# A small product behind every TensorE step of the last two pairs

## The chip, the cores and the metric

The kernel runs on one NeuronCore of a Trainium2 chip. Its metric is the time of one execution on the device in microseconds, as the median of several runs. Five engines work side by side, each in its own program order: PE (matrix products into PSUM), DVE (vector work; it and ACT read PSUM), ACT (tanh and exp), POOL (masks and elementwise products in SBUF) and SP, which issues the transfers. They are tied together by semaphores: an instruction raises one when it is done, another engine waits until it has reached a number.

## What is computed

The input is x of 16 batches, 512 rows and 128 columns, all in fp32. A first layer is attention with 16 heads of 8 columns, causal, with normalized q and k and a soft cap of the scores; its output is added to x and normalized over the row. A second layer selects 63 of the 512 rows of each batch by a learned weight, runs attention and a feed-forward layer on those rows alone, scales them by their weight, and puts them back; the result is added and normalized once more. Cut to what matters:

```python
scores = jnp.tanh(scores / SOFTCAP) * SOFTCAP          # first layer
probs  = softmax(where(causal, scores, -inf))
x      = _layernorm(x + probs_times_v @ w_o.T)
weights = (x @ router_w)[..., 0] + router_b[0]         # second layer
sel_idx = sort(top_k(weights, 64)[1][:, :63])
x1   = x_sel + attention(rmsnorm(x_sel, ln1)) @ wo
x2   = x1 + gelu(rmsnorm(x1, ln2) @ w1) @ w2
out  = zeros.at[sel_idx].set(x2 * w_sel) + x * (1 - sel_mask)
x    = _layernorm(x + out)
```

## The kernel before

The 16 batches go in 8 pairs. The body runs for p from -1 to 10; each body has 16 steps of two half-steps, and at each half-step every engine does what a table written by hand lists for it (PE_ORDER, VE_ORDER, POOL_ORDER, ACT_ORDER). An entry such as `"late.sc0@-2"` names a function and the pair, relative to p, that it works on. `run_side` (L466) goes through the entries of one half-step and leaves out those whose pair does not exist. Between them stand the scores of the first layer: `scores` (L1142) writes them into the five banks of ps_s, ACT takes them from there with tanh (L684), then exp (L696), POOL masks them (L591), and PE multiplies with v (L1165).

The last scores are made in body 7. Bodies 8, 9 and 10 hold only what is left of the pairs 6 and 7, the stages of the second layer above all. Of these the prediction uses, in their order for one pair:

- `sel_gather` (L1233): picks the selected rows by products with a one-hot matrix E, two halves of 64 rows (k), each with 4 products of 129 columns (L1240) and 4 of 16 (L1242); its result goes through DVE to hn.
- `sel_hnT` (L1264), `sel_qkv` (L1269; rows L1272 and L1275), `sel_R` (L1250, row L1255), the mask product, and `sel_qkT` (L1289, row L1293).
- `att_scores` (L1296, row L1301), `att_P` (P0T and P1T, transposes through the helper `four`, L1172), `att_PV` (PV, L1315), `att_oT` (L1322), `att_wo` (L1327), `att_h2T` (L1332), `att_w1` (w1, L1338).
- `late_w2` (w2, L1345), and `late_sc` (L1349, row L1354), the scatter of the rows back to their places: late.sc0 for the first batch, from rows 0 to 63 of ET and proc into bank ps_a, late.sc1 for the second, from rows 64 to 127 into bank ps_m.

DVE follows nearly every one of them with a copy or a scaling, and PE's next step waits for that. PSUM has eight banks: five are ps_s, one is ps_y, and ps_a and ps_m serve all other stages in turn.

A product in fp32 shows as two records in the trace, a transpose as one.

Of the kernel before, what the change touches and what calls it, by code (L numbers as in the profile page):

```python
# [15 lines left out]
B, S, D = 16, 512, 128  # L16
# [6 lines left out]
PAIRS = B // 2  # L23
# [25 lines left out]
def moments_of(tiles, tag=""):  # L49
# [45 lines left out]
PE_ORDER = (  # L95
    ["att.S1@-2"], ["prep.qk0/1@0"],
    ["prep.qk1/1@0"], ["pv.3/1@-1", "prep.v/1@0"],
    ["fin.y1T/1@-1"], ["route.wrow/0@-1"],
    [], ["att.P0@-2", "pv.0/0@0", "att.P1@-2"],
    ["att.PV@-2"], ["fin.yT/1@-1", "att.oT@-2"],  # L100
    ["att.wo@-2", "fin.wo/1@-1"], [],
    ["prep.xT/0@1", "pv.1/0@0", "att.h2T@-2"], ["att.w1@-2", "prep.qk0/0@1"],
    ["route.wrow/1@-1"], ["prep.qk1/0@1"],
# [198 lines left out]
def build(nc, x, w_q, w_k, w_v, w_o, amask, pos, router_w, router_b, wq, wk, wv, wo, w1, w2, ln1, ln2, out):  # L302
    ctx = ExitStack()
    with ctx:
        def sb(name, shape, dt=F32):
            return ctx.enter_context(nc.sbuf_tensor(name, shape, dt))

        def sem(name):
            return ctx.enter_context(nc.semaphore(name))

        ident = sb("ident", [P, P])
# [16 lines left out]
        w1_sb = sb("w1_sb", [P, F])  # L329
# [89 lines left out]
        ps_s = ctx.enter_context(nc.psum_tensor("ps_s", [P, GROUP], F32))  # L419
# [17 lines left out]
        tanh_done = sem("tanh_done")  # L437
# [19 lines left out]
        def live(n, top):  # L457
            n = n.no if isinstance(n, Batch) else n
            return not isinstance(n, int) or 0 <= n < top

        def iterations(body):

            for p in range(-1, PAIRS + 3):
                body(p)

        def run_side(order, table, p, s, half):  # L466

            for entry in order[2 * s + half]:
                name, shift = entry.split("@")
                name, _, k = name.partition("/")  # L470
                unit = Batch(p + int(shift), int(k)) if k else p + int(shift)
                if live(unit, B if k else PAIRS):
                    table[name](unit, unit.k if isinstance(unit, Batch) else None)

        def group(p, s, lag=0):

            s -= lag
            b = Batch(p, s // 8)
            return (b, b.k, s % 8) if live(b, B) else None
# [72 lines left out]
        def _(pool):  # L552
# [60 lines left out]
            def sel_zb(q, _):  # L613

                ve["late"].wait(pool, q - 1, "z1")
                for k in range(2):
                    ve["route"].wait(pool, Batch(q, k), "coef")
                    pl["sel"].done(mul(z_base[:, k], x1[:, k, :, 0:D], coef[:, k, :, None].to_broadcast([P, NT, D])),
                                   f"zb{k}", q)

            def att_kw(q, _):
                ve["sel"].wait(pool, q, "qkT")
                pe["att"].wait(pool, q - 1, "PV")
                for k in range(2):
                    pl["att"].done(mul(
                        k_wide[:, k], qkT[:, 1, None, SLOTS * k:SLOTS * k + SLOTS].to_broadcast([P, H, SLOTS]),
                        head_of[:, :, None].to_broadcast([P, H, SLOTS])), f"kw{k}", q)
# [14 lines left out]
            def body(p):  # L642
                for s in range(16):
                    g = group(p, s, 1)
                    if g:
                        b, _, gi = g
                        pool.wait_ge(exp_done, b.no * 8 + (gi + 1))

                        nc.gpsimd.tensor_tensor(pool_mark[:, gi:gi + 1], head_of[:, 0:1], head_of[:, 0:1], ALU.mult)  # L649
                        causal(gi, 0, 1, 0, P)  # L650
                        causal(gi, 0, 2, 384, P)
                        causal(gi, 0, 3, 1024, 256)
                        causal(gi, 0, 2, 1920, P).then_inc(masked, 1)
                    for half in range(2):
                        run_side(POOL_ORDER, table, p, s, half)
# [4 lines left out]
        def _(act):  # L660
# [14 lines left out]
            def body(p):  # L675
                for s in range(16):
                    g = group(p, s)
                    if g:
                        b, _, gi = g
                        for u, (c0, c1) in enumerate(UNIT):  # L680
                            act.wait_ge(scores_ready, b.no * 16 + (2 * gi + u + 1))
                            if gi >= 2 or b.at_least(1):
                                act.wait_ge(exp_done, b.no * 8 + (gi - 1))
                            nc.scalar.activation(th[:, gi % 2, c0:c1], ps_s[:, c0:c1], ACT.Tanh,  # L684
                                                 scale=1.0 / (QK_SCALE ** 2 * DH ** 0.5 * SOFTCAP))\
                                .then_inc(tanh_done, 1)
                    for half in range(2):
                        run_side(ACT_ORDER, table, p, s, half)
                    g = group(p, s, 1)
                    if g:  # L690
                        b, _, gi = g
                        act.wait_ge(tanh_done, b.no * 16 + (2 * gi + 2))

                        if gi >= 4 or b.at_least(1):
                            act.wait_ge(pv_done, b.no * 4 + (gi // 2 - 1))
                        nc.scalar.activation(pr[:, gi % 4, :], th[:, gi % 2, :], ACT.Exp, scale=SOFTCAP)\  # L696
                            .then_inc(exp_done, 1)
# [4 lines left out]
        def _(v):  # L702
# [411 lines left out]
            def body(p):  # L1114
                for s in range(16):
                    for half in range(2):
                        run_side(VE_ORDER, table, p, s, half)
# [4 lines left out]
        def _(t_):  # L1122
            mm = nc.tensor.matmul
# [18 lines left out]
            def scores(b, k, gi, u):  # L1142

                if gi > 0 or b.at_least(1):
                    t_.wait_ge(tanh_done, b.no * 16 + (2 * gi + u - 1))
                for hb_, kb in UNIT_BLOCKS[u]:
                    g, j = 2 * (gi // 4) + hb_, gi % 4
                    c = COL[(hb_, kb)]
                    last = mm(ps_s[:, c:c + S - P * kb], k_st[32 * j:32 * j + 32, k, kb, g, :],  # L1149
                              q_st[32 * j:32 * j + 32, k, kb:NT, g, :], start=True, stop=True)  # L1150
                last.then_inc(scores_ready, 1)
# [197 lines left out]
            def late_sc(q, k):  # L1349
                ve["late"].wait(t_, q, "proc")  # L1350
                bank_free(f"late.sc{k}", q)
                rows = slice(SLOTS * k, SLOTS * k + SLOTS)
                for c in range(NT):
                    last = mm(at(f"late.sc{k}")[:, P * c:P * c + P], ET[rows, P * c:P * c + P], proc[rows, :], start=True, stop=True)  # L1354
                pe["late"].done(last, f"sc{k}", q)
# [10 lines left out]
                     "att.h2T": att_h2T, "att.w1": att_w1, "late.w2": late_w2,  # L1366
                     "late.sc0": lambda q, _: late_sc(q, 0), "late.sc1": lambda q, _: late_sc(q, 1)}

            def body(p):
                for s in range(16):  # L1370
                    for half in range(2):
                        g = group(p, s, -1)
                        if g and g[2] == 0 and half == 0:
                            t_.wait_ge(turned[g[1]], g[0].pair * 32 + 32)
                        if g:
                            scores(g[0], g[1], g[2], half)
                        run_side(PE_ORDER, table, p, s, half)
            iterations(body)

# [26 lines left out]
```

## Time and profile before

| | us |
|---|---|
| median of 3 runs (lowest, highest) | 842.22 (840.51, 843.31) |
| the profiled execution | 842.46 |
| its span on the core | 840.7 |
| PE busy, share of the span | 695.8, 83% |
| DVE busy | 615.0, 73% |
| ACT busy | 609.1, 72% |
| POOL busy | 420.1, 50% |

### The profile page before, as it was taken

What the parts mean: (1) busy time and instruction counts of PE and PEld (TensorE: products, weight loads), DVE (VectorE), ACT (ScalarE), POOL (GpSimd) and SP (SyncE); (2) the same over time, 40 slices, a digit from 0 to 9 for tenths busy, and PEclk for the clock granted to TensorE, in tenths of its full rate; (3) what the DMA queues carried; (4) which work ended last, traced back from release to release, by engine and by line L of the source; (5) the groups of instructions that cost most, each with busy time, mean ns of one, the idle gap of its engine ahead of it and who ended that gap; (6) DMA issues with size and microseconds to landing.
All of it is one profiled execution on the core that took longest, in us unless ns stands there. A gap on an engine that the chain in (4) does not pass through costs nothing.

```text
span 840.7 us, 14162 instructions
## 1 busy us (share of the span) xinstructions
PE 695.8 (83%) x4976; PEld 376.2 (45%) x4976; DVE 615.0 (73%) x1781; ACT 609.1 (72%) x403; POOL 420.1 (50%) x776
## 2 busy tenths in 40 slices
PE   3387878899899989999899999998999889855752
PEld 2233434354445444544555444544464435334332
DVE  4641548677877888789877887888888886687455
ACT  0298999898879898789788978988798979700000
POOL 4253457366645754574466545665456644502101
PEclk9557877799879996999789968997799859975755
DMA  5302030306030503030303022120303030000001
GB/s 188 87 16 48 1 76 4 73 2 175 1 76 2 126 2 76 27 66 11 76 27 64 14 50 52 26 52 1 88 1 64 1 64 27 1 0 26 0 1 50
DMA packets 96904, 36.57 MB, mean 43 GB/s; under 512 B 68018, under 2 KB 94146, under 8 KB 96834
## 3 DMA queue, kind: packets, MB, share of 16 engines
q1 hardware_dynamic: 96834, 35.67, 18.2%
q8 instruction: 40, 0.66, 0.3%
q14 instruction: 30, 0.25, 0.1%
HBM read 14.69 MB, written 4.19 MB: 22 GB/s over the span
## 4 chain that ended last, share of the span: by engine, by line
PE 57%; DVE 21%; ACT 9%; issue 7%; POOL 4%; DMA 1%; DVEq 0%; POOLq 0%; ACTq 0%
PE ps_y L1165 18%; PE ps_s L1149 13%; ACT th L684 5%; ACT pr L696 4%; PE ps_m L1255 4%; PE ps_m L1196 2%; DVE junk L916 2%; PE ps_m L1240 2%; PE ps_a L1172 2%; PE ps_m L1222 1%; PE ps_m L1172 1%; DVE k_wide L1021 1%; PE ps_a L1301 1%; PE ps_a L1196 1%; DMA k_st<-st 1%
## 5 line engine op out<-in xcount | busy, mean ns | idle before, releaser
L684 ACT ACTIVATE th<-ps_s 128x1024 f32<-128x1024 f32 (+1 forms) x256 | 309.4, 1236 | 92.3 <-PE ps_s L1149 81.5
L696 ACT ACTIVATE pr<-th 128x2560 f32<-128x2560 f32 x128 | 298.7, 2334 | 0.0
L1149 PE MATMUL ps_s<-q_st,k_st 32*128 32x512 f16 (+3 forms) x1024 | 190.4, 324 | 41.1 <-ACT th L684 29.9
L591 POOL TENSOR_SCALAR_AFFINE_SELECT pr<-pr 128x256 f32<-128x256 f32 (+2 forms) x512 | 202.9, 430 | 0.0
L1165 PE MATMUL ps_y<-pr,v_aug 128*32 128x512 f32 (+3 forms) x2048 | 194.6, 531 | 2.2 <-POOL pr L591 2.2
L649 POOL TENSOR_TENSOR pool_mark<-head_of 128x1 f32<-128x1 f32 x128 | 31.2, 243 | 225.0 <-ACT pr L696 225.0
L1149 PEld LDWEIGHTS ps_s<-q_st,k_st 32*128 32x128 f16 x1024 | 78.7, 98 | 128.8 <-ACT th L684 52.0
L1165 PEld LDWEIGHTS ps_y<-pr,v_aug 128*32 128x32 f32 x2048 | 68.2, 127 | 132.2 <-issue 116.0
L606 POOL TENSOR_TENSOR st<-qk,st 128x1024 f16<-128x1024 f32 x32 | 72.8, 2296 | 21.2 <-DVE st L830 21.2
L594 POOL TENSOR_TENSOR r<-x,rw_row 128x512 f32<-128x512 f32 x16 | 18.9, 1181 | 79.0 <-DVE x L892 79.0
L916 DVE TENSOR_SCALAR_CACHE_REDUCE junk<-w_wide,x 128x512 f32<-128x512 f32 x64 | 47.6, 744 | 1.8
L670 ACT ACTIVATE hq<-hu 128x512 f32<-128x512 f32 x8 | 5.0, 624 | 47.4 <-POOL hu L594 47.4
L594 POOL TENSOR_TENSOR k_wide<-qkT,head_of 128x1024 f32<-128x1024 f32 x16 | 30.1, 1902 | 17.6 <-DVE qkT L996 17.6
L666 ACT ACTIVATE pm<-pm 128x1008 f32<-128x1008 f32 x8 | 8.4, 1045 | 41.6 <-DVE pm L1009 41.6
L923 DVE SCALAR_TENSOR_TENSOR junk<-w_wide,x,later 128x512 f32<-128x512 f32 (+1 forms) x64 | 36.9, 577 | 1.7
L594 POOL TENSOR_TENSOR st<-qk 128x1024 f32<-128x1024 f32 x16 | 30.3, 1892 | 9.5 <-DVE qk L803 9.5
L1255 PE MATMUL ps_m<-masks,E 128*64 128x512 f32 x128 | 31.0, 628 | 0.0
L840 DVE COPY y_u<-ps_y 128x512 f32<-128x512 f32 x32 | 21.9, 683 | 8.2 <-PE ps_y L1165 8.2
L1196 PE MATMUL ps_m<-wT,xT 128*128 128x256 f32 x64 | 24.4, 517 | 2.6 <-DVE w_wide L911 2.5
L662 ACT ACTIVATE turn<-red 128x128 f32<-128x128 f32 x1 | 0.3, 309 | 33.3 <-DVE red L747 33.3
L1315 PE MATMUL ps_m<-vv,k_wide 128*128 128x32 f32 x128 | 18.2, 300 | 6.3 <-DVE k_wide L1021 6.3
L1172 PE MATMUL ps_m<-ident,w_wide 128*128 128x128 f32 x96 | 16.4, 296 | 7.7 <-DVE w_wide L906 7.2
(213 smaller groups left out, 1101.3 us busy)
## 6 DMA issues: line engine op xcount, KB each, us to landing
masks<-in_L_ffn_attention_mask SPq DMA_DIRECT2D x5, 1024.0 KB, 5.9
x_in<-in_L_attn_x SPq DMA_DIRECT2D x16, 256.0 KB, 3.2
x_res<-in_L_attn_x SPq DMA_DIRECT2D x16, 256.0 KB, 3.2
result<-y_out SPq DMA_DIRECT2D x16, 256.0 KB, 2.3
w_sb<-in_L_ffn_w SPq DMA_DIRECT2D x2, 256.0 KB
q_st<-st SPq DMA_TRANSPOSE x16, 4.6
k_st<-st SPq DMA_TRANSPOSE x16, 4.8
pr<-in_L_attn_w_q SPq DMA_DIRECT2D x1, 64.0 KB, 2.0
```

Of the source, the lines that this page charges most:

```text
L591: return nc.gpsimd.affine_select(out=buf, in_=buf, compare_op=ALU.is_ge, fill=0.0, base=0, pattern=[[0, n], [1, P]] if n > 1 else [[1, P]] ...
L594: mul = lambda out, a, b: nc.gpsimd.tensor_tensor(out, a, b, ALU.mult)
L606: pl["prep"].done(nc.gpsimd.tensor_tensor(lo_parts[s], qk_twice[s], hi_parts[s], ALU.subtract), f"lo_{part}", b)
L684: nc.scalar.activation(th[:, gi % 2, c0:c1], ps_s[:, c0:c1], ACT.Tanh, scale=1.0 / (QK_SCALE ** 2 * DH ** 0.5 * SOFTCAP))\
L696: nc.scalar.activation(pr[:, gi % 4, :], th[:, gi % 2, :], ACT.Exp, scale=SOFTCAP)\
L916: step(lambda: nc.vector.tensor_scalar(junk[:, :], w_wide[:, :], x1[:, k, c, D:D + 1], 0.0, ALU.is_ge, ALU.add, accum_out=cnt_ge[:, c:c + ...
L923: step(lambda: nc.vector.scalar_tensor_tensor(junk[:, 0:n], w_wide[:, P * c:], x1[:, k, c, D:D + 1], later[:, 0:n], ALU.is_equal, ALU.mult ...
L1149: last = mm(ps_s[:, c:c + S - P * kb], k_st[32 * j:32 * j + 32, k, kb, g, :], q_st[32 * j:32 * j + 32, k, kb:NT, g, :], start=True, stop=True)
L1165: last = mm(ps_y[32 * j:32 * j + 32, P * kb:S], v_aug[:, k, kb, h, :], pr[:, gi % 4, c:c + S - P * kb], start=(q % 2 == 0 and kb == 0), st ...
L1172: last = tr(bank[:, P * c:P * c + P], src(c), ident[:, :])
L1196: last = mm(at(f"prep.qk{i}", b)[:, 2 * D * (t % 2):2 * D * (t % 2) + 2 * D], xT[:, P * t:P * t + P], wT[:, 0:2, :].rearrange("p a d -> p ...
L1255: last = mm(at("sel.R")[SLOTS * k:SLOTS * k + SLOTS, :], E[:, c, SLOTS * k:SLOTS * k + SLOTS], masks[:, k, c, :], start=(c == 0), stop=(c ...
```

## The change

PE runs one more product, `keep_clock`, behind each step that it executes in bodies 8, 9 and 10: the identity as stationary operand, 256 columns of w1_sb streamed, written to the first 256 columns of ps_s. Ahead of body 8 PE waits once until all 256 tanh instructions are done, the last readers of ps_s. Nobody reads the product, and it raises no semaphore. No other engine's instructions change.

```diff
-        def run_side(order, table, p, s, half):
+        def run_side(order, table, p, s, half, filler=None):
...
                 if live(unit, B if k else PAIRS):
                     table[name](unit, unit.k if isinstance(unit, Batch) else None)
+                    if filler:
+                        filler()
...
+            def keep_clock():
+
+                mm(ps_s[:, 0:256], ident[:, :], w1_sb[:, 0:256], start=True, stop=True)
+
             def body(p):
+                if p == PAIRS:
+                    t_.wait_ge(tanh_done, 16 * B)
                 for s in range(16):
...
-                        run_side(PE_ORDER, table, p, s, half)
+                        run_side(PE_ORDER, table, p, s, half, keep_clock if p >= PAIRS else None)
```

The order of the built programs shows 37 such products, one for each step and not for each half-step: a half-step with two or three entries gets as many, one without entries none. All lines of PE's functions stand two lower than before (L1354 is now L1356), and the product is L1373; w_sb in these rows stands for w1_sb and w2_sb, wqkv for wqkv2.

PE at the end of the last pair, before: w2, then the two scatters, with the semaphores that the first product of a step waits for.

```order
L1345 MATMUL ps_m<-w_sb,hu 128x128 [waits ve_att0]
L1345 MATMUL ps_m<-w_sb,hu 128x128 x3
L1354 MATMUL ps_a<-proc,ET 128x128 [waits ve_att0,ve_late0]
L1354 MATMUL ps_a<-proc,ET 128x128 x3
L1354 MATMUL ps_m<-proc,ET 128x128 [waits ve_late0]
L1354 MATMUL ps_m<-proc,ET 128x128 x3
```

The same place after:

```order
L1347 MATMUL ps_m<-w_sb,hu 128x128 [waits ve_att0]
L1347 MATMUL ps_m<-w_sb,hu 128x128 x3
L1373 MATMUL ps_s<-w_sb,ident 128x256
L1356 MATMUL ps_a<-proc,ET 128x128 [waits ve_att0,ve_late0]
L1356 MATMUL ps_a<-proc,ET 128x128 x3
L1373 MATMUL ps_s<-w_sb,ident 128x256
L1356 MATMUL ps_m<-proc,ET 128x128 [waits ve_late0]
L1356 MATMUL ps_m<-proc,ET 128x128 x3
L1373 MATMUL ps_s<-w_sb,ident 128x256
```

A product now stands ahead of each scatter's first instruction, also between the two, which belong to one half-step.

PE in the selection of the last pair, before: hnT, qkv, the mask product and the transposes of q and k.

```order
L1267 MATMUL ps_m<-ident,hn 128x128 [waits ve_sel0]
L1272 MATMUL ps_a<-wqkv,hnT 128x256 [waits ve_late0,ve_sel0]
L1275 MATMUL ps_a<-wqkv,hnT 128x128 x2
L1255 MATMUL ps_m<-masks,E 64x512 [waits mask_loaded,ve_sel0]
L1255 MATMUL ps_m<-masks,E 64x512 x7
L1293 MATMUL ps_a<-ident,qk_r 128x128 [waits ve_sel0]
```

The same place after:

```order
L1269 MATMUL ps_m<-ident,hn 128x128 [waits ve_sel0]
L1373 MATMUL ps_s<-w_sb,ident 128x256
L1274 MATMUL ps_a<-wqkv,hnT 128x256 [waits ve_late0,ve_sel0]
L1277 MATMUL ps_a<-wqkv,hnT 128x128 x2
L1373 MATMUL ps_s<-w_sb,ident 128x256
L1257 MATMUL ps_m<-masks,E 64x512 [waits mask_loaded,ve_sel0]
L1257 MATMUL ps_m<-masks,E 64x512 x7
L1373 MATMUL ps_s<-w_sb,ident 128x256
L1295 MATMUL ps_a<-ident,qk_r 128x128 [waits ve_sel0]
```

Each of the four steps has a product behind it; nothing is moved past anything else.

## Rows read from the trace of the kernel before

**Rows 1.** The page's granted TensorE clock, in tenths, 40 slices of 21 us.

```profile
PEclk9557877799879996999789968997799859975755
```

**Rows 2.** Stretches: length, busy us (instructions) of PE, PEld, DVE, ACT, POOL, PEclk, DMA.

```profile
750.00:760.00 10.00, 4.33 (x17) 3.74 (x17) 8.33 (x41) 0.00 (x0) 0.75 (x1) 0.50 0.01 2
760.00:770.00 10.00, 3.00 (x13) 2.33 (x12) 9.20 (x25) 0.63 (x1) 2.73 (x3) 0.50 0.00 1
```

**Rows 3.** Stretches, PE alone: length, busy us (records), PEclk, DMA share, GB/s.

```profile
776.00:778.00 2.00, 2.00 (x16) 0.50 0.00 0
778.00:780.00 2.00, 2.00 (x20) 0.61 0.00 0
784.00:786.00 2.00, 1.74 (x6) 0.50 0.00 0
```

**Rows 4.** PE timeline of the tail: start, us, what, xrecords [idle before, releaser].

```profile
775.60 1.95 PE L1240 MATMUL ps_m<-x,E 128*64 128x129 f32 x8 [1.34 <-DVE y_out L1080]
...
784.26 1.22 PE L1272 MATMUL ps_a<-wqkv,hnT 128*128 128x256 f32 x2 [0.58 <-DVE hnT L971]
785.27 1.06 PE L1275 MATMUL ps_a<-wqkv,hnT 128*128 128x128 f32 x4
786.27 5.39 PE L1255 MATMUL ps_m<-masks,E 128*64 128x512 f32 x16
...
796.62 1.98 PE L1301 MATMUL ps_a<-k_wide,qkT 128*64 128x512 f32 x4 [1.63 <-POOL k_wide L594]
...
804.12 1.12 PE L1172 MATMUL ps_a<-ident,pm 128*128 128x128 f32 x4 [3.88 <-ACT pm L666]
...
808.49 3.62 PE L1315 MATMUL ps_m<-vv,k_wide 128*128 128x32 f32 x16 [0.78 <-DVE k_wide L1021]
...
813.83 0.76 PE L1327 MATMUL ps_m<-wo,oT 128*128 128x128 f32 x2 [0.48 <-DVE oT L1034]
...
818.01 2.08 PE L1338 MATMUL ps_m<-h2T,w_sb 128*128 128x128 f32 x8 [0.45 <-DVE h2T L1051]
825.24 2.07 PE L1345 MATMUL ps_m<-w_sb,hu 128*128 128x128 f32 x8 [5.15 <-DVE hu L1065]
828.01 1.43 PE L1354 MATMUL ps_a<-proc,ET 64*128 64x128 f32 x5 [0.70 <-DVE proc L1073]
829.03 0.58 PE L1354 MATMUL ps_m<-proc,ET 64*128 64x128 f32 x1
...
829.84 1.27 PE L1354 MATMUL ps_m<-proc,ET 64*128 64x128 f32 x5
```

**Rows 5.** Stretches of earlier pairs, PE alone, columns as in Rows 3.

```profile
700.00:720.00 20.00, 18.68 (x174) 1.00 0.00 1
577.80:580.00 2.20, 2.12 (x18) 1.00 0.00 0
```

**Rows 6.** PE timeline inside those stretches, columns as in Rows 4.

```profile
704.96 1.10 PE L1240 MATMUL ps_m<-x,E 128*64 128x129 f32 x8
...
711.20 1.16 PE L1222 MATMUL ps_a<-wT,yT 128*128 128x128 f32 x8
...
718.49 0.70 PE L1272 MATMUL ps_a<-wqkv,hnT 128*128 128x256 f32 x2 [0.58 <-DVE hnT L971]
719.03 0.61 PE L1275 MATMUL ps_a<-wqkv,hnT 128*128 128x128 f32 x4
719.57 3.65 PE L1255 MATMUL ps_m<-masks,E 128*64 128x512 f32 x16
...
577.88 1.97 PE L1315 MATMUL ps_m<-vv,k_wide 128*128 128x32 f32 x16 [0.82 <-DVE k_wide L1021]
```

**Rows 7.** Timelines of ACT and of PE around the last tanh.

```profile
726.15 1.45 ACT L684 ACTIVATE th<-ps_s 128x1536 f32<-128x1536 f32 x1 [1.33 <-PE ps_s L1149]
...
733.34 1.08 PE L1301 MATMUL ps_m<-k_wide,qkT 128*64 128x512 f32 x4
```

**Rows 8.** DVE timeline: the second scatter of the pair before the last is taken over.

```profile
774.77 0.68 DVE L1080 TENSOR_TENSOR y_out<-ps_m,z_base 128x512 f32<-128x512 f32 x1
```

## The prediction

> **What bounds the kernel now.** I read the page first. Its TensorE clock row [rows 1] swings between high and half values and is low in most of the last five slices. Those are some 100 us in which the scores of all batches are done and only the last pairs' selection, attention on the selected rows and feed-forward are left. There the stages form one chain: PE makes a small product, DVE copies or scales it, PE makes the next. The ten-microsecond stretches [rows 2] say which engine ends last: from 750 to 770 DVE is busy for 8.33 and 9.20 of each 10 us, so DVE sets the pace whatever PE does. After that neither fills its time, and each product's length and each hand-over counts. The two-microsecond stretches [rows 3] show the clock: it rises only at the end of 778 to 780, behind a gather that ran back to back from 775.60 [rows 4], and is 0.50 (1.2 GHz) again at 784. The PE timeline [rows 4] gives each product of the tail with its wait, and an earlier, full stretch at 1.00 (2.4 GHz) [rows 5] gives the same forms at the high clock [rows 6].
>
> **What the change adds.** One wait and 37 products of 256 columns in fp32, on PE alone. The wait asks for the last tanh, which started at 726.15 and took 1.45; PE comes to it ahead of the product that starts at 733.34 [rows 7]: nothing. The products raise no semaphore, read two constants and write banks that nobody uses any more, so no other engine waits for them. What they cost is PE's place in line: the next real product stands behind them.
>
> *Price of one.* The same form, one fp32 product of 128 x 256, went from its start to its successor's in 785.27 - 784.26 = 1.01 us at 1.2 GHz [rows 4] and in 719.03 - 718.49 = 0.54 us at 2.4 GHz [rows 6]. A gap of G us ahead of the next real product covers that much, so a link costs about 1.0 - G at the low clock and 0.55 - G, mostly nothing, at the high one. The lower bound of a link is zero (another engine is late anyway), the upper one the whole row with its drain, 1.22 - G; I take 1.0, since the next product doesn't wait for a drain.
>
> *If the clock stayed as it is, by links, from rows 4.* h2T to w1: G is 0.45, so 0.55, twice, once in each of the two pairs that are left: 1.1. w2 to the first scatter (late.sc0): G is 0.70, so 0.3, twice: 0.6. hnT to qkv: G is 0.58, so 0.4. qkv to the mask product, and the mask product to the transposes of q and k: no gap, 1.0 each. oT to wo in the last pair: G is 0.48, so 0.5. P1T to PV: G is 0.78, so 0.2. Of the first of the two pairs, what lies before 770 and isn't named here I cost at nothing, since DVE is late there [rows 2]; without that cover it would be another 0.5 to 1.5.
>
> The dear one is between the scatters late.sc0 and late.sc1. They use different halves of the array's rows, and the records interleave: ps_m's first starts at 829.03, while the first five of ps_a run from 828.01 to 829.44, and both are done at 829.84 + 1.27 = 831.11, in 3.1 us. Eight records of that width alone take 2.08 (the w1 row). A product over all 128 rows between them ends the overlap: 2.08 + 1.0 + 2.08 = 5.1, so 2.0 more. In the last pair that is on the path whole. In the pair before, PE was done 1.34 before the gather at 775.60, at 774.26, and DVE took the second half at 774.77 [rows 8], so 0.5 was slack: 1.5. A rule bears on this: the Trainium skill (TensorE: Matmul & The Clock Gate, Part 3: Packing small matmuls) has matmuls on different row groups run concurrently, but in strict program order, the last one issued ending last and none started ahead of an earlier one. In these rows ps_m starts before ps_a's last records, so the measurement decides. By strict order there would be no overlap to lose between whole steps, the product would cost its 1.0 alone, and the sum would be 2.0 lower.
>
> Sum without a change of the clock: 1.1 + 0.6 + 0.4 + 2.0 + 0.5 + 0.2 + 2.0 + 1.5 = 8.3 us.
>
> *What the clock gives back.* (a) Before 768: whatever the clock does there, DVE is late: zero. (b) From 768 to 800: w2, product, sc0, product, sc1, product, gather, product leave no gap over a microsecond, as the gather alone did that raised the clock at 779. I expect 2.4 GHz from about 773 to 800. The gather's first half, 1.95, becomes 1.10 [rows 4, 6], and so does the second: 1.7. The scatter pair's extra 1.5 shrinks to about 0.5, since two times 1.16 (eight records, L1222) and 0.55 stand against the 3.1 and half of it is still at the low clock: 1.0. qkv, 786.27 - 784.26 = 2.01, becomes 719.57 - 718.49 = 1.08: 0.9. The products on hnT, qkv and masks shrink from 0.4, 1.0 and 1.0 to 0, 0.55 and 0.55: 1.3. The mask product goes from 5.39 to 3.65: 1.7. The scores of the selected rows (L1301) go from 1.98 to 1.08 [rows 7]: 0.9. Together 7.5. (c) P0T, P1T and PV with two products between: PV is 3.62 at the low clock and 1.97 at the high one [rows 4, 6], a gain between 0 and 1.65. PE waits 3.88 ahead of P0T, so the clock has to rise on the way: I take 1.0. (d) Behind 812 PE waits up to 5.15 at a time while POOL, ACT and DVE work; there I expect 1.2 GHz, but for part of the last scatter pair: 0.5 (bounds 0 and 2).
>
> **Sum:** 8.3 - 7.5 - 1.0 - 0.5 = -0.7 us. The profiled execution took 842.46 (its span is 840.7, and 1.8 lie around it), 0.24 above the median of 842.22; against the median this gives 841.5. A measurement of this kernel can tell about 0.3%, 2.5 us, from no change: the forecast is no change that can be told.
>
> **Rivals.** *The clock is held further.* If it rises before PV and stays up through oT, wo, h2T and w1 of the last pair, (c) is 1.65, the products there cost nothing (0.5 and 0.55), and w1 goes from 2.08 to 1.16: 0.65 + 1.05 + 0.9 = 2.6 more, so 838.9. Held to the end, w2 (0.9) and the last scatters (1.5 more) follow, 836.5. For it: P0T to PV is denser than before. Against it: the waits of 3.88 and 5.15 have one product each. By the Trainium skill (TensorE: Matmul & The Clock Gate, Part 1: The HAM clock gate) the half clock is the resting state and activity lifts it, which speaks for this case; the trace agrees in direction at 779, and shows nothing of so thin a filling.
>
> *The clock does not rise at 773, and the kernel is slower.* The price is all of the 8.3, less 1 to 3 us that the mask product and what follows regain, since qkv, product and masks now run back to back: 5 to 7 us, so 847 to 849. One thing decides it: whether PE is at 1.00 when the gather starts, around 776. For it: w2 to sc1 still has two hand-overs to DVE, and in the trace of before the clock was low until the gather was nearly over. Against it: those hand-overs are filled now.
>
> *It does not do what it says.* The words say one product for each half-step; the order shows one behind each step, also between two steps of one half-step. One for each half-step would leave the scatters overlapped and the sum about 2.5 lower, 839; the order excludes it, so it has no chance of its own.
>
> **How the numbers follow.** Forecast 0.50 (841.5; by the bounds of (c), (d) and the price, 839 to 844.5), clock held further 0.25 (836.5 to 838.9), clock not raised 0.25 (847 to 849). Leaving out a tenth at either end gives 837.5 to 848. The forecast lies almost whole within 0.3% (839.7 to 844.7): faster 0.27, same 0.48, slower 0.25.
>
> **What would show it.** Right: 74 records of the new line; a clock of 1.00 from about 774 to 800; a gather whose halves take 1.1 each and a mask product of 3.7; ps_m of both scatters starting only behind a product; a last pair that loses time behind PV. Wrong: a gather still at 1.95 a half (then slower by 5 or more), the last w1 at 1.16 (then faster by 3 or more), scatters that still interleave, or a DVE that is idle more than some 2 us in all between 750 and 768.

## The result and the profile after

The kernel got slower: 845.68 us in the median of 6 runs (843.69 to 846.38) against 842.12 for the kernel before in the same comparison (840.51 to 843.31, 6 runs), a ratio of 1.0040 with a 95% interval of 1.0025 to 1.0054. The forecast was 841.5, "no change that can be told"; the measured change, 0.25 to 0.54% to the slower side, can be told. The profiled execution took 845.58, its span is 843.9 (840.7 before).

The page of the kernel after: PE's busy row, then busy tenths and granted clock in 40 slices.

```profile
PE 716.5 (85%) x5050; PEld 390.7 (46%) x5050; DVE 614.2 (73%) x1781; ACT 609.5 (72%) x403; POOL 420.3 (50%) x776
...
PE   3388888899899989998899998998999889867864
...
PEclk9556877799779996999789978997899869975955
```

PE has 20.7 us more of work, and in the third slice from the end the clock is 0.9 where it was 0.7 [rows 1], yet the span is longer. The new line has its 74 records, two for each of 37 products:

```profile
L1373 PE MATMUL ps_s<-w_sb,ident x74: 379/483/793, 734.7 to 834.7; 128*128 128x256 f32 x74
```

**Where the 3.2 us arose.** I read the PE timelines of both kernels side by side, from one mark: the product of the selected scores into ps_m, at 733.34 before [rows 7] and at 733.72 after. It is the first step that has a product behind it. Up to it both run the same work, and it starts anywhere from 731.3 to 735.3 in the profiles of this study, so I count from it. From the mark to the end of the last scatter it was 97.77 us before (829.84 + 1.27 - 733.34) and is 100.50 after. The PE timeline of the kernel after, from w2 of pair 6 to the gather of pair 7 (the figures ahead of the shape, as in 64*128, are the rows and columns of the array that a product uses):

```profile
770.33 2.08 PE L1347 MATMUL ps_m<-w_sb,hu 128*128 128x128 f32 x8 [4.48 <-DVE hu L1067]
772.20 1.06 PE L1373 MATMUL ps_s<-w_sb,ident 128*128 128x256 f32 x2
773.19 2.07 PE L1356 MATMUL ps_a<-proc,ET 64*128 64x128 f32 x8
775.20 1.22 PE L1373 MATMUL ps_s<-w_sb,ident 128*128 128x256 f32 x2
776.35 2.07 PE L1356 MATMUL ps_m<-proc,ET 64*128 64x128 f32 x8
778.35 1.22 PE L1373 MATMUL ps_s<-w_sb,ident 128*128 128x256 f32 x2
779.50 1.98 PE L1242 MATMUL ps_m<-x,E 128*64 128x129 f32 x8
```

The scatters no longer interleave: eight records into ps_a, a product, eight into ps_m, 776.35 + 2.07 - 773.19 = 5.23 us where the pair took 3.1 before. The wait of 1.34 ahead of the gather [rows 4] is gone, and the gather starts 45.78 behind the mark instead of 42.26. Its first half still takes 1.98: the clock is not up. The stretches of the same kernel, PE alone (busy us, records, clock, DMA share, GB/s):

```profile
770.00:772.00 2.00, 1.67 (x8) 0.50 0.01 4
...
780.00:782.00 2.00, 2.00 (x17) 0.50 0.00 0
782.00:784.00 2.00, 2.00 (x20) 0.67 0.00 0
784.00:786.00 2.00, 1.49 (x8) 1.00 0.00 0
...
802.00:804.00 2.00, 0.00 (x0) 0.95 0.00 0
804.00:806.00 2.00, 1.06 (x5) 0.50 0.00 0
```

From 770.33 to 784 PE had work without a gap, at 0.50 until 783. Then 1.00 held for 20 us, to the end of the wait ahead of P0T. The timeline there and in the last pair:

```profile
789.47 3.65 PE L1257 MATMUL ps_m<-masks,E 128*64 128x512 f32 x16
...
793.81 0.60 PE L1373 MATMUL ps_s<-w_sb,ident 128*128 128x256 f32 x2
794.24 0.60 PE L1174 MATMUL ps_m<-ident,w_wide 128*128 128x128 f32 x4
...
798.33 1.08 PE L1303 MATMUL ps_a<-k_wide,qkT 128*64 128x512 f32 x4 [1.05 <-POOL k_wide L596]
...
804.93 1.11 PE L1174 MATMUL ps_a<-ident,pm 128*128 128x128 f32 x4 [3.26 <-ACT pm L668]
...
809.30 3.62 PE L1317 MATMUL ps_m<-vv,k_wide 128*128 128x32 f32 x16
...
813.96 1.06 PE L1373 MATMUL ps_s<-w_sb,ident 128*128 128x256 f32 x2
814.81 0.64 PE L1329 MATMUL ps_m<-wo,oT 128*128 128x128 f32 x2
...
819.07 1.92 PE L1340 MATMUL ps_m<-h2T,w_sb 128*128 128x128 f32 x8
...
826.14 2.08 PE L1347 MATMUL ps_m<-w_sb,hu 128*128 128x128 f32 x8 [4.71 <-DVE hu L1067]
...
829.00 2.07 PE L1356 MATMUL ps_a<-proc,ET 64*128 64x128 f32 x8
...
832.15 2.07 PE L1356 MATMUL ps_m<-proc,ET 64*128 64x128 f32 x8
```

The mask product takes 3.65 instead of 5.39 and the selected scores 1.08 instead of 1.98 [rows 4], so P0T is only 0.43 behind when counted from the mark. But P0T meets a low clock, PV stays at 3.62, and the last scatters end 5.22 us after they began. In three parts, counted from the mark: up to the gather +3.52, from the gather to P0T -3.09, from P0T to the end +2.30, together +2.73; the mark itself is 0.38 later.

### The profile page after: what moved, and what is told of

Same layout as the page of the kernel before. It is cut to its first block, busy times and chain, and to the rows that moved or that the text cites. A ratio compares the mean times of both kernels' runs of the same rounds, so it can differ in the third digit from the quotient of the medians.

```text
span 843.9 us, 14310 instructions
## 1 busy us (share of the span) xinstructions
PE 716.5 (85%) x5050; PEld 390.7 (46%) x5050; DVE 614.2 (73%) x1781; ACT 609.5 (72%) x403; POOL 420.3 (50%) x776
## 4 chain that ended last, share of the span: by engine, by line
PE 59%; DVE 21%; ACT 8%; issue 6%; POOL 4%; DMA 1%; DVEq 0%; POOLq 0%; ACTq 0%
PE ps_y L1167 18%; PE ps_s L1151 13%; ACT th L686 5%; PE ps_m L1257 3%; ACT pr L698 3%; PE ps_m L1198 2%; DVE junk L918 2%; PE ps_m L1242 2%; PE ps_a L1174 2%; PE ps_s L1373 2%; PE ps_m L1224 1%; PE ps_m L1174 1%; PE ps_a L1198 1%; DVE k_wide L1023 1%; DVE qn_v L821 1%
## 5 line engine op out<-in xcount | busy, mean ns | idle before, releaser
L1151 PE MATMUL ps_s<-q_st,k_st 32*128 32x128 f16 (+3 forms) x1024 | 189.5, 325 | 39.6 <-ACT th L686 29.8
L1373 PE MATMUL ps_s<-w_sb,ident 128*128 128x256 f32 x74 | 32.0, 525 | 0.0
L1257 PE MATMUL ps_m<-masks,E 128*64 128x512 f32 x128 | 29.2, 598 | 0.0
L849 DVE RECIPROCAL rd<-ps_m 128x32 f32<-128x32 f32 x8 | 2.9, 358 | 29.2 <-PE ps_m L1174 29.2
```

Of the source, the lines that this page charges most:

```text
L1257: last = mm(at("sel.R")[SLOTS * k:SLOTS * k + SLOTS, :], E[:, c, SLOTS * k:SLOTS * k + SLOTS], masks[:, k, c, :], start=(c == 0), stop=(c ...
L1373: mm(ps_s[:, 0:256], ident[:, :], w1_sb[:, 0:256], start=True, stop=True)
```

## The experiments

All of them place the same product by a list with one number for each of the 37 steps. The steps are, in PE's order: 0 the selected scores of pair 6 (second half); 1 to 10 the rest of its attention and the end of the first layer (1 the last product with v, 2 y turned, 3 a row step, 4 to 6 P0T, P1T and PV, 7 to 10 yT, oT, wo and the output projection of the first layer); 11 to 16 h2T, w1, a row step, w2 and the two scatters of pair 6; 17 to 26 the gather to the selected scores of pair 7; 27 to 36 its P0T, P1T, PV, oT, wo, h2T, w1, w2 and scatters. In these kernels the products are line L1381, and the other lines of PE stand as in the kernel after.

```diff
             def keep_clock():

-                mm(ps_s[:, 0:256], ident[:, :], w1_sb[:, 0:256], start=True, stop=True)
+                n = step_no[0]
+                step_no[0] += 1
+                for _ in range(COUNTS[n]):
+                    mm(ps_s[:, 0:256], ident[:, :], w1_sb[:, 0:256], start=True, stop=True)
```

The results in one table: the ratio to the kernel before in the same comparison, and from each profile the distance from the mark to the start of the gather, to P0T of pair 7 and to the end of the last scatter (start of its last row plus that row's length).

| kernel | median us | ratio (95%) | gather | P0T | end |
|---|---|---|---|---|---|
| before | 842.12 | | 42.26 | 70.78 | 97.77 |
| after: all 37 | 845.68 | 1.0040 (1.0025, 1.0054) | 45.78 | 71.21 | 100.50 |
| none between the scatters | 838.51 | 0.9953 (0.9940, 0.9966) | 43.91 | 68.59 | 94.65 |
| half rows between them | 839.67 | 0.9970 (0.9960, 0.9980) | 44.07 | 68.71 | 95.20 |
| only between the scatters | 846.65 | 1.0049 (1.0036, 1.0061) | 43.92 | 71.80 | 100.92 |
| only gather to scores | 840.25 | 0.9970 (0.9960, 0.9980) | 42.28 | 67.85 | 94.84 |
| the same, 32 columns | 842.99 | 1.0001 (0.9988, 1.0015) | 42.25 | 71.16 | 98.16 |
| only steps 0 to 10 | 843.06 | 1.0019 (0.9997, 1.0042) | 43.89 | 71.79 | 98.78 |
| only steps 27 to 36 | 843.81 | 1.0026 (0.9997, 1.0054) | 42.26 | 70.78 | 100.05 |
| 24 products, from step 11 | 838.19 | 0.9951 (0.9938, 0.9965) | 42.30 | 67.52 | 94.68 |
| all and four more | 845.27 | 1.0040 (1.0027, 1.0054) | 45.77 | 71.22 | 100.49 |
| waits filled | 834.78 | 0.9903 (0.9884, 0.9923) | 42.07 | 67.35 | 89.61 |
| filled further | 832.45 | 0.9889 (0.9874, 0.9903) | 41.26 | 64.85 | 87.56 |
| filled further, and between | 833.92 | 0.9895 (0.9874, 0.9915) | 41.57 | 65.19 | 89.41 |

**The product between the scatters.** First without the two, then with the two over 64 of the 128 rows, then with these two alone.

```diff
-COUNTS: 1 for all
+COUNTS: 1 for all but 15 and 35, 0 for these
```

> As the changed kernel, but without the two products between late.sc0 and late.sc1 (35 of 37 remain). Theory: those two take away the overlap of the scatters, 1.9 us in the pair before the last and 2.1 in the last by the timelines before and after, so about 841.6 us, and a pair that again takes 3.1; if the clock then rises before the gather is over, up to 1.7 more, near 840. Rival, the products only delay PE by their own 0.85 to 1.0 us each: about 843.7, with the two scatters still one behind the other or the loss elsewhere.

```diff
+                rows = 64 if n in (15, 35) else P
-                    mm(ps_s[:, 0:256], ident[:, :], w1_sb[:, 0:256], start=True, stop=True)
+                    mm(ps_s[:, 0:256], ident[0:rows, :], w1_sb[0:rows, 0:256], start=True, stop=True)
```

> As the changed kernel with all 37 products, but the two between the scatters use only rows 0 to 63 of the array, the half that late.sc0 uses. Theory: it is the rows that end the overlap, so late.sc1, on rows 64 to 127, starts beside the product again: the pair takes about 3.1 to 3.9 us instead of 5.2 and the kernel about 842 to 843. Rival, place in line decides (late.sc1 waits for whatever stands ahead of it): the pair stays at 5.2 and the kernel at 845.7.

```diff
-COUNTS: 1 for all
+COUNTS: 1 for 15 and 35, 0 for all others
```

> Two products in all, one between the two scatters of each of the last two pairs. Theory (a product over all rows ends the overlap of the half-row products): each pair 5.2 instead of 3.1 us, 2.1 more in the last pair, 1.5 to 1.9 more in the pair before, so 842.2 + 3.6 to 4.0 = 846. Rival (it costs its place in line alone, 0.85 each): 843.5 to 844.

Without the two products the change is a gain of 0.47%. The PE timeline of that run shows the scatters interleaved again, 772.70 + 1.27 - 770.88 = 3.09 us:

```profile
770.88 1.43 PE L1356 MATMUL ps_a<-proc,ET 64*128 64x128 f32 x5
771.90 0.58 PE L1356 MATMUL ps_m<-proc,ET 64*128 64x128 f32 x1
...
772.70 1.27 PE L1356 MATMUL ps_m<-proc,ET 64*128 64x128 f32 x5
773.90 1.22 PE L1381 MATMUL ps_s<-w_sb,ident 128*128 128x256 f32 x2
775.31 1.95 PE L1242 MATMUL ps_m<-x,E 128*64 128x129 f32 x8 [0.18 <-DVE y_out L1082]
```

With a product over half the rows the second scatter starts (774.76) before the first has run out, and the product's two records stand among those of the second scatter:

```profile
773.31 1.86 PE L1356 MATMUL ps_a<-proc,ET 64*128 64x128 f32 x7
774.76 0.58 PE L1356 MATMUL ps_m<-proc,ET 64*128 64x128 f32 x1
...
775.18 0.63 PE L1381 MATMUL ps_s<-w_sb,ident 64*128 64x256 f32 x1
...
775.77 1.06 PE L1356 MATMUL ps_m<-proc,ET 64*128 64x128 f32 x4
```

The pair takes 3.52. With the two products alone, the kernel is as slow as with all 37, and its pairs take 5.2 us. Its last pair:

```profile
828.67 2.07 PE L1356 MATMUL ps_a<-proc,ET 64*128 64x128 f32 x8 [0.70 <-DVE proc L1075]
830.67 1.22 PE L1381 MATMUL ps_s<-w_sb,ident 128*128 128x256 f32 x2
831.82 2.07 PE L1356 MATMUL ps_m<-proc,ET 64*128 64x128 f32 x8
```

In all three the pair does what the theory of the array's rows says, and the rival, a place in line like any other, falls three times. One thing the three don't separate: the full product uses all rows, and it also has another form (128*128) than the scatters (64*128), while the half-row product keeps to the scatters' rows and to their form. Which of the two ends the overlap is not shown. Two of the times lie below what was expected: 838.51 against 841.6, or near 840 with an earlier clock, and 839.67 against 842 to 843. The clock is part of that: it rose earlier, at 777.6 and at 780.0, while the gather ran, and it was up for P0T and for the last w1 (0.65 and 1.16 in the first run; 1.11 and 1.92 in the kernel after).

**What the products give back, and whether it is the clock.** Ten places, from the gather to the selected scores, with products of 256 columns and then of 32.

```diff
-COUNTS: 1 for all
+COUNTS: 1 for 17 to 26, 0 for all others
```

> Only the ten products behind the steps from the gather of the last pair to its second scores (S1). Theory: in the changed kernel the clock stood at 1.00 from 783 to 804 and that stretch won 3.0 us (the shift went from +3.9 at hnT to +0.8 at P0T), and these ten products alone do it: about 839 to 840. Rival, the clock rises there only because the products before made PE dense: no gain, about 842, or slower by their own price, 843 to 844.

```diff
+COUNTS: 1 for 17 to 26, 0 for all others
-                    mm(ps_s[:, 0:256], ident[:, :], w1_sb[:, 0:256], start=True, stop=True)
+                    mm(ps_s[:, 0:32], ident[:, :], w1_sb[:, 0:32], start=True, stop=True)
```

> The ten places from the gather to the selected scores, as in the run that has products of 256 columns there alone (840.25), but each product has only 32 columns. Tells whether the gain there comes from the clock or from the place in line. Theory (clock): the clock falls at the end of the gather as in the kernel before and rises again only within the mask product, the mask product takes 5.4 again, and the time is that of before plus at most 0.1 for each product, 842 to 843. Rival (a product in these places is enough, whatever it does): masks of 3.65 and 840.3.

With 256 columns P0T comes 2.93 us earlier from the mark (840.25; the expectation was 839 to 840); with 32 it comes 0.38 later, and the time is that of before. The PE timeline of the run with 256 columns has the mask product at the high clock,

```profile
787.69 3.65 PE L1257 MATMUL ps_m<-masks,E 128*64 128x512 f32 x16
```

and that with 32 columns, in the same place of the program, at the low one:

```profile
786.06 5.26 PE L1257 MATMUL ps_m<-masks,E 128*64 128x512 f32 x16
```

Both stand behind a product; what differs for them is the clock. The stretches of the narrow run show 1.00 at 780 to 782 and 0.50 from 784 to 788, as before [rows 3]; as before, it rises again only while the mask product runs. So the gain is the clock's.

**The first stretch and the last.** Steps 0 to 10 alone, and 27 to 36 alone.

```diff
-COUNTS: 1 for all
+COUNTS: 1 for 0 to 10, 0 for all others
```

> Only the eleven products behind the steps from att.S1 to fin.wo of the pair before the last, up to about 754 us. Theory: this stretch is not covered by DVE as the forecast assumed; it alone makes everything behind it 2.0 us late, as the shift of h2T showed, so about 844.1 unless a later clock change gives some back. The forecast's step, DVE is late there anyway: no difference, 842.1.

```diff
-COUNTS: 1 for all
+COUNTS: 1 for 27 to 36, 0 for all others
```

> The ten products behind P0T and the later steps of the last pair alone, the one between its scatters among them. Theory: the clock falls in the waits of 3.88 and 5.15 whatever stands behind the steps, PV keeps 3.62, and the scatter pair of 5.2 instead of 3.1 and small links cost what they cost in the change from P0T on, 2.3: 844.5. Rival (two products raise the clock for PV, and the 1.0 of the forecast is gained): 843.3 or less.

Neither median can be told from that of before at 95%, both lie above it (+0.19%, +0.26%), so the traces decide. With 0 to 10 alone h2T and w2 of pair 6 and the gather come 1.63 later from the mark, the whole of what the kernel after lost up to h2T (1.62); later 0.6 of it is regained, since the clock is up during part of the mask product (4.39). With 27 to 36 alone nothing moves up to P0T, PV keeps 3.62, and the end is 2.28 later, as in the kernel after (2.30). The rival, that the thin filling raises the clock for PV, falls.

What the first stretch hits shows on DVE. Its timeline before (start, us, operation, wait and releaser):

```profile
748.53 0.29 DVE L1034 COPY oT<-ps_m 128x128 f32<-128x128 f32 x1 [0.63 <-PE ps_m L1322]
```

and after:

```profile
750.49 0.29 DVE L1036 COPY oT<-ps_m 128x128 f32<-128x128 f32 x1 [2.21 <-PE ps_m L1324]
```

PE's steps from PV to oT run back to back there, so each product between them delays oT; DVE waits 2.21 instead of 0.63, and the work that keeps DVE full from 750 on [rows 2] starts that much later.

**Without the first stretch and the scatters.**

```diff
-COUNTS: 1 for all
+COUNTS: 0 for 0 to 10, 15 and 35, 1 for all others
```

> 24 of the 37 products: the eleven behind the steps from the last scores up to the output projection of the pair before the last are left out, and so are the two between the scatters. Theory: without the eleven, PE comes to h2T 1.6 us earlier against S1 than with them (the delay that the run with those eleven alone showed), so the time lies 1.6 us below the run without products between the scatters (838.5): 837. Rival: the eleven bring activity that helps the clock to rise earlier at the gather (there it rose 2.3 us behind the gather's start, with the products of 768 to 800 alone 4.1 us behind it); without them the clock rises 1.8 us later, a gather half costs 0.85 more and the gain is eaten up: 838.5 or more.

In the trace the gather comes 1.6 earlier from the mark than with steps 0 to 10, as the theory had it, and the end no earlier. The time, 0.9951, is that of the run with them (0.9953): a miss. In this profile the clock was up at 774 already, while the interleaved scatters ran, but it fell at 784, behind the waits that follow the gather: the mask product took 4.59, and P0T and the last w1 took 1.12 and 1.92 where the run with steps 0 to 10 has 0.65 and 1.16. The stretches, columns as above:

```profile
772.00:774.00 2.00, 2.00 (x13) 0.56 0.62 170
774.00:776.00 2.00, 1.29 (x10) 1.00 0.00 0
...
780.00:782.00 2.00, 0.78 (x6) 1.00 0.00 0
...
784.00:786.00 2.00, 2.00 (x8) 0.50 0.00 0
```

The profiled execution, 840.37, is the slowest of its five, but its mark is also late: 734.34 against 731.40 in the run with steps 0 to 10, which is the whole difference to the profiled execution there (837.42). What the clock did in the other four I can't say. The steps from 0 to 10 cost 1.6 where they stand; whether they help later is left open.

**A clock that is up before the scatters.** All 37 products and four more behind the row step ahead of w2.

```diff
-COUNTS: 1 for all
+COUNTS: 5 for 13, 1 for all others
```

> The change with all its 37 products, the two between the scatters among them, and four products more behind the row step ahead of w2 in the pair before the last. Theory (the step that failed is the clock's rise at 773, and with it up there the rest of the sum holds): 1.00 from about 769; w2 takes 1.16 instead of 2.08 (0.9 less), the scatter pair with its product 2.9 instead of 5.2 (2.3 less), the gather up to 1.7 less: 845.7 - 3.2 to 4.9 = 840.8 to 842.5. Rival (the clock falls again in the two waits between w2 and the gather, or the scatters cost their 5.2 at any clock): 844.5 to 845.7.

The time and every distance in the table are those of the kernel after: the rival holds. Its timeline:

```profile
762.98 2.32 PE L1381 MATMUL ps_s<-w_sb,ident 128*128 128x256 f32 x10
768.07 2.08 PE L1347 MATMUL ps_m<-w_sb,hu 128*128 128x128 f32 x8 [2.76 <-DVE hu L1067]
```

The five met a high clock, were done in 2.32, and left a wait of 2.76; the clock fell in it, and w2 and the scatters ran at 0.50 as before. So this run does not try the forecast's sum at a high clock, it repeats the low one; the filled runs below leave 1.1 to 1.3 of the same wait, and there w2 takes 1.16.

**Waits filled.** Then I filled PE's long waits, in two steps, without the products between the scatters and without the first stretch (in the second step five products stand at its end), and put those between the scatters back in a third.

```diff
-COUNTS: 1 for all
+COUNTS: 0 for 0 to 10, 15, 28 and 35; 5 for 13; 6 for 26 and 33; 2 for 27; 1 for all others
```

> As the run with 24 products, but the long waits of PE are filled: five products behind the row step ahead of w2, six behind the selected scores, two behind P0T and none behind P1T, six behind w1 of the last pair. Theory (the clock falls in PE's own waits, and a filled wait keeps it): 1.00 from the scatters or the gather through PV, so that PV takes 1.97 instead of 3.62 and the last w2 and scatters are at the high clock too (0.9 and 0.5): 1.65 + 0.9 + 0.5 = 3 less than 837, 834. Rival: the products that stand in a wait are themselves late where the clock is low (0.85 each), six of them overrun the wait of 3.3 us behind the selected scores by 1.8, and the time is 838 to 839.

```diff
-COUNTS: 0 for 0 to 10, 15, 28 and 35; 5 for 13; 6 for 26 and 33; 2 for 27; 1 for all others
+COUNTS: 0 for 0 to 9, 15, 28 and 35; 5 for 10 and 13; 2 for 14 and 34; 4 for 16; 6 for 26; 3 for 27 and 31; 9 for 33; 1 for all others
```

> The run with filled waits, filled further: five products ahead of h2T of the pair before the last, two behind each w2, four behind the scatters of the pair before, three behind P0T and behind the output projection of the last pair, nine behind its w1. Theory (a filled wait keeps the clock up, and the products end within it): the gather's two halves take 1.1 each (1.27 and 1.50 before), 1.0 less up to the turn of E, and w1 of the pair before and the products on oT are at the high clock, 0.5 to 1.3 less: 834.8 - 1.5 to 2.3 = 832.5 to 833.3. Rival: where the clock is low the products overrun their waits (nine at 0.85 are 7.7 in a wait of 5.3, four at 0.85 are 3.4 in one of 2.8), which costs up to 3: 836 to 838.

```diff
-COUNTS: 0 for 15 and 35
+COUNTS: 1 for 15 and 35
```

> The further filled run (832.45) with the two products between the scatters put back. Tells what such a product costs where the clock is up. Theory (the scatters stand one behind the other at either clock, and the high one halves the price): 1.16 + 0.55 + 1.16 = 2.9 or a little less instead of the 1.7 from 771.33 to 773.04, 1.1 more in each pair, of which 0.5 may be slack in the first: 832.45 + 1.6 to 2.2 = 834.0 to 834.7. Rival (without the interleaving the clock does not hold through the scatters and falls to 0.50 before the gather, as it was 0.50 through all of them in the change): 2 more at the gather and up to 1 in the last pair, 836.5 or more.

The first takes 1.0% off the kernel before (834.78, expected 834), the second 1.1% (832.45 against 842.24, expected 832.5 to 833.3); both beat the kernel before and the kernel after, and both rivals fall. The PE timeline of the second:

```profile
771.33 0.82 PE L1356 MATMUL ps_a<-proc,ET 64*128 64x128 f32 x5 [0.55 <-DVE proc L1075]
...
772.32 0.72 PE L1356 MATMUL ps_m<-proc,ET 64*128 64x128 f32 x5
...
775.76 1.07 PE L1242 MATMUL ps_m<-x,E 128*64 128x129 f32 x8 [0.80 <-DVE y_out L1082]
...
803.26 2.41 PE L1317 MATMUL ps_m<-vv,k_wide 128*128 128x32 f32 x16 [0.78 <-DVE k_wide L1023]
...
812.45 4.05 PE L1381 MATMUL ps_s<-w_sb,ident 128*128 128x256 f32 x18
817.77 1.16 PE L1347 MATMUL ps_m<-w_sb,hu 128*128 128x128 f32 x8 [1.27 <-DVE hu L1067]
```

The gather's half takes 1.07, w2 1.16, and PV 2.41, since the clock fell within it. The products end inside their waits: nine behind w1 leave 1.27 of 5.15. The last scatters of the third:

```profile
820.12 1.16 PE L1356 MATMUL ps_a<-proc,ET 64*128 64x128 f32 x8 [0.55 <-DVE proc L1075]
...
821.83 1.16 PE L1356 MATMUL ps_m<-proc,ET 64*128 64x128 f32 x8
```

With a product between them the pair takes 822.99 - 820.12 = 2.87 instead of 1.71 (772.32 + 0.72 - 771.33; the last pair takes the same), so at the high clock such a product costs 1.16 in the last pair; in pair 6 the gather moves by 0.3 only. That is 1.5, just under the 1.6 to 2.2 that the theory allowed; the medians differ by 1.47 too, but the ratios to the kernel before overlap, so this rests on the traces. By the table the end moves by 1.85: another 0.35 came between P0T and the last scatters, where the clock fell earlier within PV (2.73 instead of 2.41). The clock held through the serial scatters, and the rival falls.

## Why the prediction was wrong

The forecast was -0.7 us. By its own terms, cut at the gather and at P0T and set against the trace:

| stretch | forecast | measured |
|---|---|---|
| up to the gather | +1.35 | +3.52 |
| gather to P0T | -4.1 | -3.09 |
| P0T to the end | +2.05 | +2.30 |

- **What the change adds.** Right: 74 records, no other engine's work, and the wait for the last tanh costs nothing that shows (the mark moves 0.38, within its 4 us of scatter between profiles).
- **The price of one product.** 1.0 and 0.54 were a little high: between two steps of its own form it is 814.81 - 813.96 = 0.85 at the low clock and 794.24 - 793.81 = 0.43 at the high one. Beside steps of another form it is more: 773.19 - 772.20 = 0.99 ahead of the first scatter, 779.50 - 778.35 = 1.15 between the second scatter and the gather. The small links were over-costed: h2T to w1 grew by 0.20 instead of 0.55, w2 to the first scatter by 0.08 instead of 0.3.
- **"What lies before 770 and isn't named here I cost at nothing, since DVE is late there", and clock term (a).** This step failed: +1.62. DVE is busy from 750 on, but it starts that work when PE's oT and wo are there, and ahead of oT it was waiting for PE (0.63) even before the change. A busy engine hides nothing that stands ahead of its own start. The prediction had named the bound without this cover, 0.5 to 1.5. Its sign for this, a DVE idle more than some 2 us between 750 and 768, came (18 - 14.67 = 3.33), but the kernel before was over it already (2.47).
- **The scatters.** The mechanism was right, and it was the dearest single part: 5.2 us, +2.1 in the last pair (forecast 2.0). In pair 6 it was +1.88 of the time from the first scatter to the gather, where the clock was to bring 1.5 down to 0.5. Strict program order, the rule of the Trainium skill that the prediction set against its rows (TensorE: Matmul & The Clock Gate, Part 3: Packing small matmuls), would have left no overlap to lose; the runs without, with half, and with nothing but these products agree with the rows.
- **"I expect 2.4 GHz from about 773 to 800", term (b).** This step failed by ten microseconds: 783 to 804. The scatters kept their full price (1.0 missed), and the gather gained nothing (1.7 missed). What follows the gather came as forecast, a mask product of 3.65 and scores of 1.08.
- **Terms (c) and (d).** PV kept 3.62: 1.0 missed. The clock fell in the wait of 3.26 with one product in it; with six products there it stayed up (the filled runs). One product doesn't always lose it: without the products between the scatters the clock outlasted the same wait and fell behind P0T. For the last scatters 0.5 was missed too. The smaller price of the links between made up for most of it.
- **The rivals.** The second named the very point, PE's clock when the gather starts, and it came true; 847 to 849 was 1 to 3 us too much. From the gather to P0T its price without the clock was 2.4 (0.4, 1.0 and 1.0), and the stretch came out at -3.09, so 5.5 came back there, where the rival allowed 1 to 3; the links behind P0T cost less too, and the 1.62 of the first stretch, which it did not have, took part of that away. "Clock held further" did not happen: the last w1 took 1.92.

Not settled is what decides the moment at which the clock rises. With the same filling from h2T on, but for the products between the scatters, it was up at 774 in the run with 24 products, at 777.6 without the two between the scatters, at 780.0 with half rows between them, and at 783 in the kernel after, where the scatters stood one behind the other; but serial scatters did not bring a clock down that was up. Whether their serial form delayed the rise was not tried by itself. The kernel before itself took 832.0 and 831.78 us in two of its executions, at a mean clock of 0.836 instead of 0.824. Neither has a trace, so I can't say where the clock differed; it needed no product for it.

## What to carry to other kernels

A product that nobody reads is not free on an in-order engine: ask at each place whether the next real step is already waiting for PE, and put fillers only into PE's own waits, enough to leave little of the wait and few enough to end before the operand comes. Never put a product over all rows between two that share the array by halves. Count an engine's busy share as cover only from the moment at which its work no longer starts on the delayed one.

## What the runs showed of the hardware

- Products on different halves of the array's rows overlapped (3.1 us for the pair at 1.2 GHz, 1.7 at 2.4). One product over all rows between them ended that (5.2 and 2.9), one of their own form over the half that was running did not (3.5).
- The clock can stay at 0.50 for 13 us of PE work without a gap (770.33 to 783 in the kernel after), and it fell within waits of 2.76 and 3.26 that had been partly filled, but outlasted the one of 3.26 in two other runs (P0T at 0.65 and 0.66). The Trainium skill (TensorE: Matmul & The Clock Gate, Part 1: The HAM clock gate) has the half clock as the resting state that activity lifts; the direction agrees, as the runs with narrow and wide products in the same places show (mask products of 5.26 and 3.65). What sets the moment no run here shows.
